# A decoder layer on one core: the order in which the attention part hands its tasks to PE, ACT, DVE and POOL

## What is computed

```python
x = _layernorm(x + _L0_attn_ref(x, Wq, Wk, Wv, proj_w, proj_b))       # 16 heads of 64, causal
x = _layernorm(x + _L0_xattn_ref(x, ctx, ctx, mask, w_q, w_k, w_v, w_o))  # 16 heads of 16, 77 keys
x = _layernorm(x + _L0_ffn_ref(x, Wr, W1, b1, W2, b2, fw1, fb1, fw2, fb2))  # 8 experts, top 2
```

## Time and profile before

| | us |
|---|---|
| median of 3 runs | 1456.32 (1455.64 to 1457.85) |
| the profiled execution's own time | 1455.44 |
| its span in the trace | 1453.7 |
| PE busy | 1288.9 (89%) |
| DVE busy | 1081.1 (74%) |
| ACT busy | 922.0 (63%) |
| POOL busy | 731.8 (50%) |

### The profile page before, as it was taken

One profiled execution on the slowest core, in us unless ns is written; L12 is line 12 of the kernel. 1 busy time (PEld: TensorE's weight loads), 2 busy tenths in 40 slices (PEclk: granted clock), 3 DMA queues, 4 the chain that ended last, 5 costly groups with the idle time before them and its releaser, 6 DMA issues. The chain is left out here.

```text
span 1453.7 us, 47504 instructions
## 1 busy us (share of the span) xinstructions
PE 1288.9 (89%) x16821; PEld 1081.1 (74%) x16821; DVE 1081.1 (74%) x3112; ACT 922.0 (63%) x2383; POOL 731.8 (50%) x974
## 2 busy tenths in 40 slices
PE   4899999999999999999999998736999999999930
PEld 3788888887888888888888887513788888888820
DVE  4898899888888988988988988566455555555537
ACT  4677878777787887887888776304444444444436
POOL 4435666565566566566566453411243434444326
PEclk9999999999999999999999999965999999999975
DMA  9756767776776776767777654068233363333345
GB/s 242 132 101 137 160 148 188 166 155 150 200 158 144 204 154 156 180 172 154 159 197 160 130 112 76 23 253 338 61 70 80 102 164 75 74 74 75 70 157 201
DMA packets 292449, 208.96 MB, mean 144 GB/s; under 512 B 218782, under 2 KB 249630, under 8 KB 289792
## 3 DMA queue, kind: packets, MB, share of 16 engines
q1 hardware_dynamic: 278784, 180.87, 52.2%
q0 software_dynamic: 7136, 18.76, 4.5%
q10 hardware_dynamic: 6304, 6.29, 1.5%
HBM read 93.79 MB, written 65.93 MB: 110 GB/s over the span
## 5 line engine op out<-in xcount | busy, mean ns | idle before, releaser
L1784 PE MATMUL ps_e<-xt,wres 128*128 128x128 f16 x3408 | 343.4, 220 | 6.1 <-DMA xt<-xg 5.1
L1784 PEld LDWEIGHTS ps_e<-xt,wres 128*128 x3408 | 284.9, 98 | 78.3 <-issue 6.8
L1848 ACT ACTIVATE act_g<-ps_e,b 128x128 f32<-128x128 f32 x568 | 161.8, 368 | 208.6 <-PE ps_e L1784 208.6
L1791 PE MATMUL ps_e<-wres,g_hi 128*128 x568 | 214.6, 379 | 0.8 <-DVE g_lo L1871 0.8
L753 ACT ACTIVATE probs<-st_k,nmax 128x128 f32<-128x128 f32 (+1 forms) x512 | 202.3, 452 | 17.3 <-DVE nmax L1003 17.3
L1751 POOL DMA_INDIRECT z_scr<-e_y,dst_i x71 | 85.1, 1198 | 210.2 <-DVE e_y L1862 206.9
L1003 DVE CUSTOM_DVE_ANT_0 st_k<-ps,causal 128x128 f32<-128x128 f32 (+1 forms) x512 | 160.7, 351 | 31.9 <-ACT probs L753 16.5
L760 ACT ACTIVATE pt_hi<-ps 128x384 f16<-128x384 f32 x256 | 124.9, 488 | 59.1 <-PE ps L460 57.1
L1320 POOL TENSOR_TENSOR o_st<-o_norm,o_st 128x256 f16<-128x256 f32 x128 | 86.0, 672 | 149.7 <-ACT o_st L768 149.5
L1793 PE MATMUL ps_e<-wres,g_lo 128*128 x568 | 154.9, 273 | 0.0
L1008 DVE TENSOR_TENSOR pt_lo<-ps,pt_hi 128x384 f16<-128x384 f32 x256 | 140.9, 550 | 16.8 <-ACT pt_hi L760 15.6
(11 more groups left out here) (285 smaller groups left out, 3981.7 us busy)
## 6 DMA issues: line engine op xcount, KB each, us to landing
k_pair<-k_pair SPq DMA_DIRECT2D x96, 256.0 KB, 6.4
st_p<-in_moe_w SPq DMA_DIRECT2D x24, 768.0 KB, 6.7
w_scr<-st_p SPq DMA_DIRECT2D x24, 768.0 KB, 5.0
wres<-w_scr SPq DMA_DIRECT2D x18, 1024.0 KB, 22.7
v_scr<-v_tok SPq DMA_DIRECT2D x32, 512.0 KB, 4.3
v_pos<-v_scr SPq DMA_DIRECT2D x64, 256.0 KB, 6.1
q_st<-st_q SPq DMA_DIRECT2D x64, 128.0 KB, 2.8
z_scr<-zero SPq DMA_DIRECT2D x32, 256.0 KB, 5.2
```

Of the source, the lines that this page charges most:

```text
L1784: last = mm(out, w(c * FF + f * P, b, P), xt[:, t % X_BUFS, a, c], start=(m == 0), stop=(m == 5))
L1791: mm(out[:, 0:2 * D], g_hi[:, t % G_BUFS, f], w(KC * FF + f * D, 0, 2 * D), start=(f == 0), stop=False, skip_group_check=True)
L1848: nc.scalar.activation(act_g[:, k % 2, f], ps[:, 3 + 2 * (k % 2) + f // 4, (f % 4) * P:(f % 4 + 1) * P], ACT.Gelu, bias=bias[:, f:f + 1], ...
```

## The change

The calls in the `step` functions of PE, ACT, DVE and POOL are written in another order; no task is added, dropped or altered inside. Part of the difference in the text is only where a `step` begins: the list is rotated, and a call with s becomes one with s - 1 or s + 3. What is left, for a tile T in the middle of the program:

- ACT: `exps(T+1, 0)` and `exps(T+1, 1)` move up; `stage_c(T, 0)`, which fills `o_t`, now stands ahead of `piece_high(., 0)` and `hi(., 3)` instead of behind them; `hi(., 2)` moves down, behind `exp2(., 1)` and `stage_c(., 7)`; the pieces of weights stand together; `exps(T, 4)` and `exps(T, 5)` move up by one place, `o_high(T, 1)` by three, `hi(., 1)` by one.
- PE: `scores(T+1, 0)` ahead of `fill(., 2)`; `pv2(., 1)` ahead of `scores(., 3)`; `value_rows(., 0)` ahead of `stage_d(., 1)` and `stage_d(., 2)` ahead of `value_rows(., 1)`; `turn_probs(., 3)` ahead of `scores(., 5)`; `scores(., 6)` and `scores(., 7)` ahead of `turn_probs(., 4)` and `(., 5)`; `stage_d(., 4)` behind `pv(., 3)`.
- DVE: `lo(., 1)` behind `maxima(., 0)`, `lo(., 2)` behind `stage_c(., 7)`, `pt(., 0)` ahead of `stage_d(., 0)` and `lo(., 3)`, `maxima(., 4)` ahead of `pt(., 1)`, `moments` of the second norm ahead of `pt(., 2)`, `normalise(., 1)` ahead of `lo(., 4)`, `maxima(., 7)` ahead of `normalise(., 3)`, which with `pt(., 5)` is now ahead of `stage_d(., 4)`.
- POOL: `split_x` ahead of the pieces, `bias_x` and `split_context` at the end of a tile's turn, `own_values(., 0)` ahead of `split_x2`.
- At the start: `late_split(0)` on ACT ahead of `hi(0, 4)`, and the causal mask behind `fill(0, 5)` and `hi(0, 5)`.

```diff
@@ PE, step @@
             if has(s - 1):
                 turn_probs(s - 1, 7)
+            if has(s):
+                scores(s, 0)
             if has(s + 1):
                 fill(s + 1, 2)
-            if has(s):
-                scores(s, 0)
...
             if has(s):
                 turn_probs(s, 0)
+            if has(s - 2):
+                pv2(s - 2, 1)
+            if has(s):
                 scores(s, 3)
-            if has(s - 2):
-                pv2(s - 2, 1)
...
@@ ACT, step @@
+            if has(s):
+                exps(s, 1)
+            if has(s - 1):
+                stage_c(s - 1, 0)
             if 0 <= s - 4 < PIECES:
                 piece_high(s - 4, 0)
+            if has(s):
+                pt(s, 0)
             if has(s + 1):
                 hi(s + 1, 3)
             if has(s - 1):
-                stage_c(s - 1, 0)
+                stage_c(s - 1, 1)
             if 0 <= s - 4 < PIECES:
                 piece_up(s - 4, 0)
                 piece_high(s - 4, 1)
...
@@ DVE, step @@
             if has(s):
                 maxima(s, 1)
             if has(s - 2):
                 stage_c(s - 2, 7)
             if s == 1:
                 late_split(7)
+            if has(s + 1):
+                lo(s + 1, 2)
```

More of the change, by code:

```diff
@@ L620, in step @@
         def step(s):
+            if has(s - 2):
+                stage_c(s - 2, 4)
+                if s - 1 == TILES:
+                    stage_c(s - 2, 6)
+            if has(s - 1):
+                scores(s - 1, 6)
+            if s == 0:
+                causal_mask()
+            if has(s - 1):
+                turn_probs(s - 1, 4)
+            if has(s + 1):
+                fill(s + 1, 0)
+            if has(s - 1):
+                pv(s - 1, 3)
+            if has(s - 3):
+                stage_d(s - 3, 4)
+            if has(s - 1):
+                scores(s - 1, 7)
+                turn_probs(s - 1, 5)
+            if has(s - 2):
+                stage_c(s - 2, 5)
+            if has(s - 1):
+                pv(s - 1, 4)
+                turn_probs(s - 1, 6)
+                pv(s - 1, 5)
+            if has(s - 2):
+                if s - 1 != TILES:
+                    stage_c(s - 2, 6)
             if has(s + 1):
@@ L685, in step @@
                 stage_d(s - 2, 3)
[L686 to L709, removed]
         def causal_mask():
@@ L887, in step @@
                 pt(s, 1)
[L888 to L893, removed]
+            if 0 <= s - 4 < PIECES:
+                piece_high(s - 4, 2)
             if has(s):
@@ L1411, in step @@
-            if has(s - 2):
-                own_values(s - 2, 0)
-                shift(s - 2, 0)
+                inverse_deviation(s + 1, 0, s_mv1, s_rstd1)
+            if has(s + 1) and even(s + 1):
+                spread_k2(s + 1, 1)
+            if s == -3:
+                constants()
+            if 0 <= s - 2 < PIECES:
+                piece_low(s - 2, 2)
+            if has(s):
+                inverse_deviation(s, 1, s_mv2, s_rstd2)
+            if has(s + 1):
+                own_values(s + 1, 0)
@@ new lines, in step @@
+            if has(s):
+                split_x2(s)
+            if has(s + 1):
+                shift(s + 1, 0)
+            if has(s + 2):
+                bias_x(s + 2)
+            if has(s + 2) and even(s + 2):
+                split_context(half(s + 2))
+            if has(s + 2):
+                split_o(s + 2, 1)
+            if has(s + 1):
+                own_values(s + 1, 1)
+            if has(s + 2):
+                split_o(s + 2, 3)
+            if has(s + 1):
+                shift(s + 1, 1)
@@ L1415, in _ @@
+            if has(s + 2):
+                split_o(s + 2, 5)
         pool.sem_inc(s_w_out, 16)
```

252 lines of the change are left out of this document (112 added, 140 removed).

## The result

| | before | changed |
|---|---|---|
| median, runs on one chip | 1457.24 us (8) | 1448.9 us (8) |
| lowest to highest | 1455.64 to 1459.59 | 1444.35 to 1453.96 |
| profiled execution, span | 1455.44, 1453.7 | 1453.96, 1452.2 |
| PE busy, 100 to 900 us | 767.87 | 780.24 |
| tile length, odd and even | 26.85, 28.31 | 26.69, 28.15 |

The ratio of the times is 0.9943 [0.9925, 0.996]: 8.3 us less, where 7.9 were forecast. The changed kernel's runs spread over 9.6 us, those of before over 4, and its profiled execution was the slowest of its eight, only 1.5 us better than that of before. So a difference of these two traces understates the change, and one has to ask where the profiled execution lost.

The account below looks back on a forecast made before the run. PE, then DVE from `q_lo` on, was taken to bound each tile. The sum -9.5 + 0.6 + 1.0 = -7.9 us gave 1447.5 for the profiled execution and 1448.4 us as median, range 1443.5 to 1454.

Parts of the forecast that it names:

- The bound: Tile length is PE's list up to `q_lo` on DVE, and DVE's list from there to PE's `stage_c(., 6)`.
- the first rival: PE's line 460 waits for DVE shrink too: 19.5 us more, 1429; likelier 0.1 to 0.2 a tile, about 1444; chance 0.10.
- the prediction's signs: Among them: PE's line 460 waits remain, fewer ahead of `turn_probs(., 4)`, longer ahead of `(., 6)`; `scores(0, 0)` still at about 35.
- `o_t` ahead of the piece, -9.5: On ACT, `o_t` no longer waits behind twelve late loads of weight pieces; 9.5 us go.
- `o_t` itself in time, 0: ACT is ready for `o_t` half a microsecond earlier, then PE's transposes set its start; price nothing, 0.5 us in hand.
- PE's and DVE's swaps, 0 a tile: Reordered tasks on PE and DVE change nothing; bounds -0.1 to +0.1 a tile, -3 to +3 us in 31 tiles.
- the prediction's own sign: Tile length 26.9 us in every odd tile and 28.3 in every even one; prediction wrong if tiles are shorter.
- Late queries, +0.6 with bounds 0 to 3: SP's queue slips with `v_out` 1.75 us later while `scores(., 0)` comes 1.3 sooner; two tiles' queries late, 0.6 us.
- The start, +1.0: First tile: `fill(1, 2)` comes behind `scores(0, 0)` and pushes `maxima(0, 2)` by 0.4 to 1.9 us; +1.0 taken.
- the start costs more: Rival: 3 to 5 us, two fills at half clock and a first tile that stays behind: 1451 to 1453; chance 0.06.
- The remark drawn from the Trainium skill: PE's clock gate defaults to throttled, so `fill(1, 2)` and `fill(1, 3)` may run at half clock: 1.9 instead of 1.0 us.
- POOL slows DVE: Rival: POOL's moved tasks slow one instruction of DVE's leading stretch, 6 to 12 us: 1454 to 1461; chance 0.03.

Follow-up runs that it names:

- e6_ot_split_x: Kernel before with ACT's `o_t` write ahead of `piece_high(., 0)` and `hi(., 3)`, and POOL's `split_x` ahead of the pieces: 1451.72 us, 0.9956 of before.
- e9_split_x_back: Changed kernel with POOL's `split_x` moved back between the second piece and the first norm's inverse deviation: 1481.58 us, 1.0158 of before.
- e13_pair_back: Changed kernel with the old order around `scores(., 0)` on PE, DVE and ACT in all tiles: 1446.16 us, 0.9928 of before.
- e11_start_pe: Changed kernel with only PE's `fill(1, 2)` and `fill(2, 2)` ahead of `scores(0, 0)` and `scores(1, 0)` again: 1446.59 us, 0.9922 of before.
- e7_after_again: Changed kernel run once more, unedited: 1449.86 us, 0.9941 of before.
- e1_ot_only: Kernel before with only ACT's `stage_c(., 0)`, the write of `o_t`, ahead of `piece_high(., 0)` and `hi(., 3)`: 1466.14 us, 1.0052 of before.

## Why the prediction was right, and where it was not

- **The bound** (PE's list up to `q_lo`, then DVE's) held: in the changed kernel PE's gap only moved, the stretch from `stage_c(., 4)` to `stage_c(., 6)` kept its length, and the first rival's 19.5 us did not come. It moved to line 553, `stage_c(., 5)`, and not to line 460 ahead of `turn_probs(., 6)`, where the prediction's signs had put it.
- **`o_t` ahead of the piece, -9.5:** the size was right. The late pieces had cost 9.7 us in the tile lengths, and they are gone. But the term was booked as if ACT's swap alone brought it. Alone it costs 7.6 us. The step that failed is the sentence "In the new order `o_t` has the piece behind it, and these 9.5 us go", together with the look at what the late piece holds up: I named `pt(., 0)` on ACT and never followed the piece to POOL, where `piece_low` waits for it and the inverse deviation stands behind. The change's POOL part, which the prediction has no term for, is what makes it pay (`e6_ot_split_x`, `e9_split_x_back`). A forecast for the ACT edit alone, by the same reasoning, would have been 17 us off.
- **`o_t` itself in time, 0:** right. ACT is ready 0.31 us before PE's transposes are.
- **PE's and DVE's swaps, 0 a tile:** wrong, and outside the bounds. A tile is 0.16 us shorter, 5 us in all, against -3 as the lower bound. They did not come from DVE's stretch behind `q_lo`, to which the bounds belonged, but from `scores(., 0)` with `lo(., 1)` and `lo(., 2)`, which stand where I had priced only SP's queue: `e13_pair_back` has the 26.84 of before. By the prediction's own sign, tiles shorter than 26.9 and 28.3 us, this part of it is wrong. The first rival's likelier form, 0.1 to 0.2 us a tile, had the size, but from `turn_probs(., 4)`, which `e13_pair_back` leaves in the new order.
- **Late queries, +0.6 with bounds 0 to 3:** the mechanism was right and the size small: 2.3 us, and about 2.5 in two further executions, 5.7 in `e11_start_pe`. The margin is 1.3 us in most tiles, and the landing time varies by more than that (2.7 to 4.6 us in one execution).
- **The start, +1.0:** the largest error. 4 us in the medians, 3.5 and 7.65 in the two executions, which differ mostly by how long the transfers of keys and queries took to land. The step that failed took `fill(1, 2)` as six matmuls that delay `maxima(0, 2)`, and did not follow `lo(1, 2)` into SP's list to `v_out(1)` and the queries of tile 1. The prediction had used just this path for the tiles in the middle. The rival "the start costs more" (3 to 5 us) was right in size, for another reason than the one given: half a clock is only a part of it. The remark drawn from the Trainium skill ("TensorE: Matmul & The Clock Gate", the section on the HAM clock gate) has the trace on its side: `fill(1, 2)` took 2.56 us behind 4.88 us of idle time, where the full clock gives 1.3, and `fill(2, 2)` did the same behind 3.81 us, and in `e7_after_again` behind 1.40 us.
- **POOL slows DVE, a rival with 0.03:** not in the changed kernel, where the first norm's median is 452 ns against the 461 of the earlier trace rows, with the same longest, 805. But it is in `e1_ot_only`, where that median is 799 and the longest 1239 ns.

The sum by what was measured, for an execution like `e7_after_again`: -9.7 for the pieces, -5.0 for the tiles, +3.4 for late queries and single longer tiles, +3.5 for the start: -7.8, and its span is 7.9 us below that of before. That -7.9 had been forecast is in part luck: +5 too little at the start and the queries stood against -5 not foreseen in the tiles.

## What to carry to other kernels

When a task is moved to let another go first, follow what it produces into every engine's list and read what stands behind its consumer there; an engine that is half idle can still be the one that must not be late. A swap that costs time alone may be half of a pair, so try both halves together before giving it up, and take one half out of a tuned order only with the other. And price the first tiles by themselves, through the DMA queue, since what is hidden in the steady state is bare there.

## What the runs showed of the hardware

A DVE norm from SBUF to SBUF (128x256, float32) took 0.41 us by itself and 1.24 us when a POOL operation of 1.16 us had started 0.07 us ahead of it: it ended 0.15 us behind POOL's. The Trainium skill ("SBUF — State Buffer", the section on who interferes with whom) counts `tensor_scalar` among the DVE operations that can contend with GpSimd for their shared port pair, and has the later of the two wait for the whole instruction. The trace agrees in all 12 odd tiles with a piece of `e1_ot_only`. A tile in which DVE started just ahead of POOL instead isn't in these runs.

DMA transfers of one kind, 128 KB within SBUF, landed in 2.7 us at best, 2.8 in the median and 4.6 at worst in one execution. Two executions of the same program differed by 4.1 us in their first 90 us alone. 1.4 of them were there when `v_out(1)` was issued, and 2.5 came from transfers of keys and queries that landed later; both had the half clock behind them, over 2.56 us of matmuls that take 1.3 at the full one.
